# One block for a whole transformer layer: the output projection joined to attention, feed-forward weights into freed buffers

## The chip, the core and the metric

The kernel runs on one core of a Trainium2 chip. The core has five engines that work through their own instruction lists: TensorE (PE in the profile) multiplies matrices, VectorE (DVE), ScalarE (ACT) and GpSimd (POOL) work element by element, SyncE (SP) issues transfers here. They wait for each other through semaphores. The metric is device time in microseconds (us) of one execution.

## The reference, cut to what matters

```python
# x: 2 x 1024 x 512, 32 heads of 16, feed-forward width 1376, all float32
x = x + _layernorm(attention(_layernorm(x)))
x = x + _layernorm(feed_forward(_layernorm(x)))
# attention: q, k, v from w_attn, rope, causal softmax, y = probs @ v,
#            y += gating * softmax(q @ ak) @ av  (10 adapter tokens), then y @ w_proj.T
# feed_forward: (silu(x @ W_gate.T) * (x @ W_up.T)) @ W_down.T
```

## The kernel before, in words

Every matrix product that needs float32 precision is made of three: both operands are split into a high part and a low part, and high times high, high times low and low times high are added (lines 72 to 74, `split_matmuls`). ACT mostly makes the high part with a copy, DVE the low part with a subtraction.

The kernel has four stages. `stage_inputs` normalizes x and makes q, k, v and the adapter's part (`ya`) in four blocks of 512 rows. `stage_attention` goes through 16 groups of four heads; PE makes row maxima ahead of time, scores (L917) and products with v (L931), ACT takes the exponentials (L800), POOL masks the diagonal (L773). The two stages share one block of code. Each group ends with a copy of the unnormalized sums to DRAM (`y_heads`), whose last row of each head is the softmax's denominator. In the attention stage the four operand buffers `q_op`, `k_op`, `vg` are used in turn by the groups.

`stage_project` has a block of its own, so all engines meet at a barrier ahead of it. It works on 8 pieces of 256 rows. For piece m the steps are, in order:

- **load**: SP loads `y` (four transfers), two slices of the feed-forward weights (`raw`, 520 KB each), the adapter's part `ya_sb`, and x (`xr`).
- **spread** (PE, L1161): the inverse denominators `inv`, times a matrix of ones (`heads`), give a full tile `ps_r`; **divide** (DVE, L1124) multiplies y by it.
- **add** (POOL, L1079) adds the adapter's part; **high** (ACT, L1099) and **low** (DVE, L1136) split y into `y_h` and `y_l`.
- **project** (PE, L72 to L74): 24 matmuls into `ps_o`.
- **statistics** (DVE, L1143 to L1151), **power** (POOL, L1083 and L1085) for one over the deviation, **normalize** (ACT, L1113) into `z`, **residual** (POOL, L1090, z plus x), **store** (SP) to `x1` in DRAM.

Beside that ACT (L1105) and DVE (L1128) split two weight slices with every piece, so that after 8 pieces all 33 column blocks of the feed-forward weights are in `w_ffn_high` and `w_ffn_low`. `ps_r`, `ps_o`, `y`, `y_h`, `y_l` and `z` have two buffers each. The steps are written as a software pipeline, and DVE does for each turn: statistics of the piece before, divide of the next, two weight slices, low of the next.

`stage_feed_forward` is another block behind another barrier. It takes four blocks of 512 rows, the first of them straight from `z`. DVE and POOL normalize it, PE transposes it into `ps_f` (L1388), ACT and DVE split it (L1278, L1326), and then for each of 11 slices f PE makes `ps_g`, `ps_u` and the part of `ps_d` from the slice before. The next block's front is made beside that.

## Time and profile before

| | us |
|---|---|
| median of 3 runs (lowest, highest) | 1250.85 (1249.85, 1255.54) |
| the profiled execution | 1256.06 |
| its span, first to last instruction | 1254.4 |
| PE busy in the span | 1134.4 |
| DVE busy | 713.2 |
| ACT busy | 515.3 |
| POOL busy | 266.7 |

All durations in this document's prediction come from the profiled execution. A busy PE isn't a PE at its best: matmul ends are modelled, and the granted clock (1.00 is 2.4 GHz, 0.50 is 1.2 GHz) is shown apart. Times of an instruction are counted from the span's start. Behind a row of the timeline stands in brackets how long the engine had been idle before it, and what released it.

### The profile page before, as it was taken

What the parts mean: (1) busy time and instruction counts of PE and PEld (TensorE: products, weight loads), DVE (VectorE), ACT (ScalarE), POOL (GpSimd) and SP (SyncE); (2) the same over time, 40 slices, a digit from 0 to 9 for tenths busy, and PEclk for the clock granted to TensorE, in tenths of its full rate; (3) what the DMA queues carried; (4) which work ended last, traced back from release to release, by engine and by line L of the source; (5) the groups of instructions that cost most, each with busy time, mean ns of one, the idle gap of its engine ahead of it and who ended that gap; (6) DMA issues with size and microseconds to landing.
All of it is one profiled execution on the core that took longest, in us unless ns stands there. A gap on an engine that the chain in (4) does not pass through costs nothing. (4 is left out here: it accounts for less than half of the span.)

```text
span 1254.4 us, 18586 instructions
## 1 busy us (share of the span) xinstructions
PE 1134.4 (90%) x7036; PEld 770.0 (61%) x7036; DVE 713.2 (57%) x955; ACT 515.3 (41%) x1058; POOL 266.7 (21%) x260
## 2 busy tenths in 40 slices
PE   3999999898999999999999976775999999999996
PEld 1878778544545455545554335654887887887884
DVE  4756747767888788777876107972324324324324
ACT  3233233246777777777776533432111112111111
POOL 3525538101311112111111103651001001001001
PEclk9999999668999999999998677886999999999998
DMA  6356786544434445544400037962001101101100
GB/s 237 91 148 178 162 179 168 104 103 77 79 78 78 79 88 96 95 82 83 92 27 19 18 101 210 291 200 100 1 1 35 66 1 38 65 1 36 66 1 34
DMA packets 82522, 113.10 MB, mean 90 GB/s; under 512 B 24964, under 2 KB 42500, under 8 KB 82436
## 3 DMA queue, kind: packets, MB, share of 16 engines
q1 hardware_dynamic: 80580, 108.21, 33.6%
q10 hardware_dynamic: 1856, 3.71, 1.7%
q8 instruction: 58, 0.95, 0.3%
q14 instruction: 28, 0.23, 0.1%
HBM read 68.83 MB, written 42.21 MB: 89 GB/s over the span
## 5 line engine op out<-in xcount | busy, mean ns | idle before, releaser
L800 ACT ACTIVATE prob<-ps_s 128x512 f32<-128x512 f32 (+3 forms) x768 | 323.2, 497 | 167.6 <-PE ps_s L917 160.6
L820 DVE TENSOR_REDUCE neg<-ps_m 128x2 f32<-128x1024 f32 (+2 forms) x224 | 248.2, 1145 | 62.0 <-PE ps_m L882 40.0
L917 PE MATMUL ps_s<-q_op,k_op 50*128 50x512 f32 (+2 forms) x768 | 249.8, 459 | 18.0 <-ACT prob L800 13.2
L917 PEld LDWEIGHTS ps_s<-q_op,k_op 50*128 50x128 f32 x768 | 122.2, 196 | 125.3 <-ACT prob L800 60.9
L882 PE MATMUL ps_m<-k_op,q_op 48*128 48x512 f32 (+2 forms) x768 | 185.6, 420 | 9.8 <-DVE neg L820 6.8
L773 POOL TENSOR_SCALAR_AFFINE_SELECT prob<-prob 128x512 f32<-128x512 f32 x128 | 81.2, 634 | 429.3 <-ACT prob L800 429.3
L931 PE MATMUL ps_y<-prob,vg 128*17 128x512 f32 (+3 forms) x1536 | 160.9, 542 | 0.0
L1342 DVE TENSOR_TENSOR hf<-sl,ps_u 128x512 f32<-128x512 f32 (+1 forms) x44 | 30.2, 686 | 190.7 <-PE ps_u L74 190.7
L820 DVE TENSOR_REDUCE neg_far<-ps_m 128x4 f32<-128x512 f32 (+2 forms) x96 | 100.2, 1048 | 29.4 <-PE ps_m L887 27.9
L1411 PE MATMUL ps_d<-w_ffn_high,wp_high 128*128 128x512 f32 (+1 forms) x352 | 115.5, 391 | 0.0
L882 PEld LDWEIGHTS ps_m<-k_op,q_op 48*128 48x128 f32 x768 | 97.0, 198 | 28.9 <-DVE neg L820 20.1
L887 PE MATMUL ps_m<-causal_h,ident_h 64*128 64x128 bf16 x1024 | 99.6, 232 | 0.0
L931 PEld LDWEIGHTS ps_y<-prob,vg 128*17 128x17 f32 x1536 | 37.2, 102 | 81.8 <-issue 39.6
L1293 ACT ACTIVATE wp_high<-hf 128x512 fp32r<-128x512 f32 (+1 forms) x44 | 27.8, 632 | 131.5 <-DVE hf L1342 131.5
L1290 ACT ACTIVATE sl<-ps_g 128x512 f32<-128x512 f32 (+1 forms) x44 | 26.2, 596 | 133.7 <-PE ps_g L74 133.6
L1411 PEld LDWEIGHTS ps_d<-w_ffn_high,wp_high 128*128 128x128 f32 (+1 forms) x352 | 66.1, 188 | 15.0
L72 PE MATMUL ps_g<-x2T_h,w_ffn_high 128*128 128x512 f32 (+1 forms) x176 | 71.9, 408 | 2.2 <-DVE wp_low L1326 1.5
L72 PE MATMUL ps_u<-x2T_h,w_ffn_high 128*128 128x512 f32 (+1 forms) x176 | 70.0, 398 | 0.9 <-DVE hf L1342 0.9
L74 PE MATMUL ps_g<-x2T_h,w_ffn_low 128*128 128x512 f32 (+1 forms) x176 | 70.3, 399 | 0.0
L74 PE MATMUL ps_u<-x2T_h,w_ffn_low 128*128 128x512 f32 (+1 forms) x176 | 69.3, 394 | 0.0
L1411 PE MATMUL ps_d<-w_ffn_low,wp_high 128*128 128x512 f32 (+1 forms) x176 | 68.9, 392 | 0.0
L1266 POOL TENSOR_TENSOR d_rs<-d_ve,minus_half 128x4 f32<-128x4 f32 x4 | 4.0, 1006 | 275.8 <-DVE d_ve L1365 275.8
(161 smaller groups left out, 1757.5 us busy)
## 6 DMA issues: line engine op xcount, KB each, us to landing
raw<-in_w_ffn SPq DMA_DIRECT2D x16, 520.0 KB, 6.3
y_heads<-y_sb SPq DMA_DIRECT2D x32, 256.0 KB, 2.1
k_op<-k_parts SPq DMA_DIRECT2D x28, 256.0 KB, 4.3
q_op<-q_parts SPq DMA_DIRECT2D x56, 128.0 KB, 5.0
v_groups<-v_out SPq DMA_DIRECT2D x16, 272.0 KB, 4.1
x<-in_x SPq DMA_DIRECT2D x4, 1024.0 KB, 7.9
q_parts<-part_h SPq DMA_DIRECT2D x16, 256.0 KB, 2.9
q_parts<-part_l SPq DMA_DIRECT2D x16, 256.0 KB, 2.9
```

Source lines behind the costliest of these rows:

```text
L72: nc.tensor.matmul(out, lh, rh, start=k == 0, stop=False)
L74: last = nc.tensor.matmul(out, ll, rh, start=False, stop=k == len(pairs) - 1)
L773: pool.affine_select(out=diag, in_=diag, compare_op=ALU.is_ge, fill=0.0, base=0, pattern=[[0, HG], [1, P]], channel_multiplier=-1).then_in ...
L800: act.activation(prob[:, v % NPROB, h, unit_cols(u)], ps_s[:, y % NS, unit_cols(u)], ACT.Exp, scale=D ** -0.5).then_inc(s_exp, 1)
L820: nc.vector.tensor_reduce(to[:, :, pairs[0]:pairs[-1] + 1, i - TT * c], scores, axis=AX.X, op=ALU.max, negate=True).then_inc(a_read, 1)
L882: last = nc.tensor.matmul(ps_m[:, g % 2, s, base:base + wide], q_op[buf][r, c, pair, (i - TT * c) * P:(i - TT * c + 1) * P], k_op[buf][r, ...
L887: last = nc.tensor.matmul(ps_m[:, g % 2, s, diag:diag + P], ident_h[r, half], causal_h[r, half], start=False, stop=half == 1)
L917: nc.tensor.matmul(ps_s[:, y % NS, lo:BLK], k_op[buf][r, pair, j * P:(j + 1) * P], q_op[buf][r, c, pair, lo:BLK], start=True, stop=True)\
L931: last = nc.tensor.matmul(ps_y[32 * h:32 * h + VW, unit_cols(u)], vg[n % NBUF][:, j, h * VW:(h + 1) * VW], prob[:, v % NPROB, h, unit_cols ...
L1293: act.activation(hT_h[0:w, s], hf[0:w, s], ACT.Copy).then_inc(h_high[s], 1)
L1342: nc.vector.tensor_tensor(hf[0:w, s], sl[0:w, s], ps_u[0:w], op=ALU.mult).then_inc(h_mul[s], 1)
L1411: last = nc.tensor.matmul(ps_d[:, tt], a[0:w, s, q], b[0:w, cols], start=f == j == 0, stop=f == NF - 1 and j == 2)
```

## The change

The whole kernel becomes one block without barriers, and the loops of the last two stages are written out. `stage_project` is cut up: its steps become methods of a class `Tail`. Pieces 0 to 3 (the first batch) are written at the end of the attention stage's lists, pieces 4 to 7 in a new `stage_project`.

- Weights are loaded in 33 pieces of 128 columns (256 KB). 0 to 11 are loaded on SP in the last three groups, and split on DVE alone (a copy and a subtraction), each set of four in the operand buffer that a group has freed. 12 to 19 go beside pieces 4 to 7, two for each, 20 to 32 beside the first feed-forward block, on ACT and DVE.
- The first batch's `y`, `ya`, x and denominators are loaded on SP in group 13; its inverses are taken and placed in group 14.
- Normalize moves from ACT to DVE; the residual is shared by POOL and DVE, half each.
- Pieces 0 to 3 all use one `ps_r` and one `ps_o`; pieces 4 to 7 use two in turn.
- DVE finishes pieces 0 and 1 two turns late (`finish(m - 2)`). From piece 3 on the statistics of a piece come in the same turn as its project.
- The second batch's inverses are loaded, taken and placed between pieces 2 and 4.
- The first feed-forward block is now rows 0 to 511, read back from DRAM into `x1_first`, and its normalization is done beside piece 6.

```diff
 # stage_attention, SP, in the loop over the groups n
+            if n == NG - 3:
+                sp.wait_ge(wp_low, 1)
+                for i in range(4):
+                    tail.load_weights(sp, i)
...
+                tail.load_sums(sp, 0)
+                tail.load_y(sp, 0)
+                tail.load_y(sp, 1)
+                tail.load_ya(sp, 0)
+                tail.load_x(sp, 0)
+            if n == NG - 1:
+                for i in range(8, 12):
+                    tail.load_weights(sp, i)
...
+            if n == NG - 2:
+                tail.place_inverses(sp, 0)
+                for i in range(4, 8):
+                    tail.load_weights(sp, i)
 # stage_attention, POOL, behind the last group
+        for m in range(NP // B):
+            tail.add_adapter(pool, m)
+            if m:
+                tail.inverse_deviation(pool, m - 1)
+                tail.residual_pool(pool, m - 1)
 # stage_attention, DVE, behind the last maximum
+        tail.invert(dve, 0)
+        def weights(group, pieces):
+            dve.wait_ge(pv, NU * (group + 1))
+            for i in pieces:
+                tail.weights_high(dve, i)
+                tail.weights_low(dve, i)
+        def finish(m):
+            tail.statistics(dve, m)
+            tail.normalize(dve, m)
+            tail.residual_dve(dve, m)
+        weights(NG - 4, range(4))
+        weights(NG - 3, range(4, 8))
+        weights(NG - 2, range(8, 12))
+        for m in range(NP // B):
+            tail.divide(dve, m)
+            if m > 1:
+                finish(m - 2)
+            tail.low(dve, m)
+        finish(2)
 # stage_attention, PE, behind the last product
+        for m in range(NP // B):
+            for half in range(2):
+                tail.spread(pe, m, half)
+            if m:
+                for part in range(4):
+                    tail.project(pe, m - 1, part)
 # class Tail
+    def load_x(self, sp, m):
+        if m:
+            sp.wait_ge(self.x1_pool, m)
+            sp.wait_ge(self.x1_dve, m)
...
+    def store_x1(self, sp, m):
+        sp.wait_ge(self.x1_pool, m + 1)
+        sp.wait_ge(self.x1_dve, m + 1)
...
+    def spread(self, pe, m, half):
+        if half == 0:
+            pe.wait_ge(self.inv_in, 16 * HB * (m // (NP // B) + 1))
+            back = 1 if m <= NP // B else 2
+            if m > NP // B or 0 < m < NP // B:
+                pe.wait_ge(self.y_div, m - back + 1)
...
+    def project(self, pe, m, part):
+        k, half = divmod(part, 2)
+        if part == 0:
+            pe.wait_ge(self.y_low, m + 1)
+            back = 1 if m <= NP // B else 2
+            if m > NP // B or 0 < m < NP // B:
+                pe.wait_ge(self.z_norm, m - back + 1)
...
 # the new stage_project, SP
+        tail.load_x(sp, 3)
+        tail.load_y(sp, 5)
+        tail.load_ya(sp, 4)
+        tail.place_inverses(sp, 1)
+        tail.store_x1(sp, 3)
+        tail.load_x(sp, 4)
+        tail.load_weights(sp, 12)
+        tail.load_weights(sp, 13)
...
 # POOL
+        tail.inverse_deviation(pool, 3)
+        tail.add_adapter(pool, 4)
+        tail.residual_pool(pool, 3)
...
 # ACT
+        for m in last_m:
+            for i in range(2 * (m - 4) + 12, min(2 * (m - 4) + 14, LATE_WEIGHTS)):
...
+                tail.weights_high_act(act, i)
+            tail.high(act, m)
...
 # DVE
+        tail.invert(dve, 1)
+        tail.statistics(dve, 3)
+        tail.normalize(dve, 3)
+        tail.residual_dve(dve, 3)
+        tail.divide(dve, 4)
+        for m in last_m:
+            for i in range(2 * (m - 4) + 12, min(2 * (m - 4) + 14, LATE_WEIGHTS)):
+                tail.weights_low(dve, i)
+            tail.low(dve, m)
+            if m + 1 < NP:
+                tail.divide(dve, m + 1)
+            if m == NP - 2:
+                tail.f_stats(dve, 0)
+            tail.statistics(dve, m)
+            if m == NP - 2:
+                tail.f_normalize(dve, 0)
+            tail.normalize(dve, m)
+            tail.residual_dve(dve, m)
+            if m == NP - 1:
+                for c in range(CC):
+                    tail.f_low_of(dve, 0, c)
```

How instructions stand in a row is shown at three places. The first is DVE in the middle of the projection. Before (one turn of the written loop; `w_ffn_low` are the weights, `y_l` is low, `p_st` to `p_ve` the statistics, `y<-y,ps_r` divide; register work left out by starting behind it):

```order
456 L1143 BN_STATS p_st<-ps_o 128x6 [waits o_step,o_ps1]
457 L1143 BN_STATS p_st<-ps_o 128x6
458 L63 REGISTER_ALU [waits z_ready1]
459 L1148 BN_AGGR p_mv<-p_st 128x2 [waits o_step]
460 L1148 BN_AGGR p_mv<-p_st 128x2
461 L1149 REGISTER_ALU
462 L1150 TENSOR_SCALAR p_mm<-p_mv 128x2 [waits o_step]
463 L1151 TENSOR_SCALAR p_ve<-p_mv 128x2
464 L1123 REGISTER_ALU [waits y_in1]
465 L1124 TENSOR_TENSOR y<-y,ps_r 128x1024 [waits over_ps]
466 L1126 ISA
467 L1128 ISA [waits f_high]
```

The changed kernel's DVE in piece 5 (`z<-ps_o` is normalize, `z<-z,xr` DVE's half of the residual):

```order
504 L1181 TENSOR_TENSOR w_low_2192<-raw,w_high_2191 128x512 [waits fw_high_act]
505 L1181 TENSOR_TENSOR w_low_2194<-raw,w_high_2193 128x512 [waits fw_high_act]
506 L1137 TENSOR_TENSOR y_l<-y,y_h 128x1024 [waits y_high]
507 L1133 TENSOR_TENSOR y<-y,ps_r 128x1024 [waits over_ps,y_in0]
508 L1145 BN_STATS p_st<-ps_o 128x6 [waits o_step,o_ps]
509 L1145 BN_STATS p_st<-ps_o 128x6
510 L1150 BN_AGGR p_mv<-p_st 128x2 [waits o_step]
511 L1150 BN_AGGR p_mv<-p_st 128x2
512 L1152 TENSOR_SCALAR p_ve<-p_mv 128x2 [waits o_step]
513 L1160 TENSOR_SCALAR z<-ps_o,p_mv,p_rs 128x512 [waits x1_out1,o_rstd]
514 L1160 TENSOR_SCALAR z<-ps_o,p_mv,p_rs 128x512
515 L1168 TENSOR_TENSOR z<-z,xr 128x512 [waits xr_in,z_norm]
```

Normalize and half of the residual now stand between the statistics of a piece and the low part of the next, and the statistics wait for the project of the same turn. The second place is SP between the batches, in the changed kernel:

```order
422 L1089 DMA ya_sb<-ya 128x4x256 [waits y_sum]
423 L1123 DMA inv<-sums 32x512 [waits inverse]
424 L1123 DMA inv<-sums 32x512
425 L1100 DMA x_dram<-z 128x2x512 [waits x1_dve,x1_pool]
426 L1095 DMA xr<-in_x 128x2x512 [waits x1_dve,x1_pool]
427 L1108 DMA raw<-in_w_ffn 128x4x128 [waits fw_low] x2
428 L1265 DMA x_first<-x_dram 128x4x512 [waits x1_out1,x1_out0]
```

Weight pieces 12 and 13 (row 427) stand behind the store of piece 3, which waits for POOL's and DVE's residual. The third is POOL there:

```order
103 L1194 TENSOR_TENSOR p_rs<-p_ve,minus_half 128x2 [waits z_norm,o_var]
104 L1188 TENSOR_TENSOR y<-y,ya_sb 128x1024 [waits yad_in,y_div]
105 L1201 TENSOR_TENSOR z<-z,xr 128x512 [waits xr_in,z_norm]
106 L1188 TENSOR_TENSOR y<-y,ya_sb 128x1024 [waits yad_in,y_div]
107 L1194 TENSOR_TENSOR p_rs<-p_ve,minus_half 128x2 [waits z_norm,o_var]
108 L1201 TENSOR_TENSOR z<-z,xr 128x512 [waits xr_in,z_norm]
```

Piece 3's half residual (row 105) stands behind piece 4's add, which waits for divide.

## Rows read from the trace of the kernel before

**Rows 1.** Stages: stretch, length, busy us (count) by engine, clock, DMA share, GB/s
```profile
690.00:738.00 48.00, 45.09 (x222) 16.05 (x221) 3.35 (x1) 26.63 (x66) 7.61 (x12) 0.68 0.05 17
738.00:865.00 127.00, 79.35 (x277) 61.15 (x274) 87.67 (x98) 40.08 (x45) 55.65 (x33) 0.77 0.66 204
```

**Rows 2.** Timeline of PE, attention's end to first project: start, us, instruction, idle
```profile
735.68 2.35 PE L931 MATMUL ps_y<-prob,vg 128*17 128x512 f32 x32
741.29 6.88 PE L1161 MATMUL ps_r<-inv,heads 96*128 96x256 f32 x16 [3.27 <-PEq L1485]
759.60 0.80 PE L72 MATMUL ps_o<-wp_high,y_h 128*128 128x512 f32 x1 [11.43 <-DVE y_l L1136]
```

**Rows 3.** Timeline of PE, last project to first feed-forward matmul
```profile
843.64 0.40 PE L74 MATMUL ps_o<-wp_high,y_l 128*128 128x512 f32 x1
...
861.18 1.97 PE L1388 MATMUL ps_f<-ident,z 128*128 128x128 f32 x8 [0.56 <-DVE wp_low L1326]
864.64 0.79 PE L72 MATMUL ps_g<-x2T_h,w_ffn_high 128*128 128x512 f32 x1 [1.49 <-DVE wp_low L1326]
```

**Rows 4.** Timeline of DVE across attention's end, and SP's first projection load
```profile
714.22 3.35 DVE L860 RECIPROCAL sums<-sums 64x512 f32<-64x512 f32 x1 [31.19 <-DMA sums<-y_heads]
...
741.26 2.68 SPq L1036 DMA_DIRECT2D y<-y_heads  x4
```

**Rows 5.** Groups by shape, 738 to 865: busy, mean ns, idle before, releaser
```profile
L1128 DVE TENSOR_TENSOR w_ffn_low<-raw,w_ffn_high 128x1040 f32 x12 | 27.5, 2334 | 0.0
...
L1143 DVE BATCH_NORM_STATS2 p_st<-ps_o 128x6 f32<-128x512 f32 x16 | 10.3, 681 | 5.5 <-PE ps_o L74 5.5
L1124 DVE TENSOR_TENSOR y<-y,ps_r 128x1024 f32<-128x1024 f32 x8 | 9.8, 1219 | 31.8 <-DMA y<-y_heads 31.8
L1099 ACT ACTIVATE y_h<-y 128x1024 fp32r<-128x1024 f32 x8 | 8.5, 1059 | 19.4 <-POOL y L1079 19.4
...
L1083 POOL TENSOR_TENSOR p_rs<-p_ve,minus_half 128x2 f32<-128x2 f32 x8 | 5.7, 708 | 25.1 <-DVE p_ve L1151 25.1
L1128 DVE TENSOR_TENSOR w_ffn_low<-raw,w_ffn_high 128x1040 fp32r<-128x1040 f32 x4 | 5.0, 1242 | 4.9 <-ACT w_ffn_high L1105 4.8
```

**Rows 6.** Single lines: duration min/median/max in ns, first and last start, form
```profile
L1136 DVE TENSOR_TENSOR y_l<-y,y_h x8: 1152/3200/3259, 758.4 to 833.4; 128x1024 fp32r<-128x1024 f32 x8
...
L1079 POOL TENSOR_TENSOR y<-y,ya_sb x8: 2361/2979/3229, 753.9 to 829.3; 128x1024 f32<-128x1024 f32 x8
...
L1270 POOL TENSOR_TENSOR inv<-inv x4: 1260/1288/1297, 964.5 to 1246.5; 128x512 f32<-128x512 f32 x4
```

**Rows 7.** Timeline of DVE: normalizing in the feed-forward stage, and the residual
```profile
856.62 1.92 DVE L1320 TENSOR_SCALAR z<-z,f_mv,f_rs 128x512 f32<-128x512 f32 x4 [1.23 <-POOL f_rs L1261]
...
963.54 1.53 DVE L1370 TENSOR_SCALAR inv<-ps_d,d_mv,d_rs 128x512 f32<-128x512 f32 x2 [1.22 <-POOL d_rs L1266]
965.20 1.16 DVE L1375 TENSOR_TENSOR inv<-inv 128x512 f32<-128x512 f32 x1
```

**Rows 8.** Timeline of PE: project behind a wait, and behind hardly any
```profile
793.46 0.80 PE L72 MATMUL ps_o<-wp_high,y_h 128*128 128x512 f32 x1 [3.19 <-DVE y_l L1136]
...
801.64 1.89 PE L1161 MATMUL ps_r<-inv,heads 96*128 x8
804.32 0.50 PE L72 MATMUL ps_o<-wp_high,y_h 128*128 128x512 f32 x1 [0.79 <-DVE y_l L1136]
...
810.00 1.24 PE L1161 MATMUL ps_r<-inv,heads 96*128 x5
...
815.09 0.50 PE L72 MATMUL ps_o<-wp_high,y_h 128*128 128x512 f32 x1 [3.20 <-DVE y_l L1136]
...
822.31 1.89 PE L1161 MATMUL ps_r<-inv,heads 96*128 x8
```

**Rows 9.** DMA issues: how often, KB each, median us from issue to landing
```profile
raw<-in_w_ffn SPq DMA_DIRECT2D x16, 520.0 KB, 6.3
...
k_op<-k_parts SPq DMA_DIRECT2D x28, 256.0 KB, 4.3
```

863 lines of the change are left out of this document (462 added, 401 removed).

## The prediction

> **What bounds the kernel now.** I read the stages first [rows 1], then the timeline at the stages' ends [rows 2, 3], then the groups and single lines inside the projection [rows 5, 6], because the change leaves the instructions of the stages ahead of and behind it as they are, and PE is the bound there. Between the last attention product's end (735.7 + 2.35 = 738.0) [rows 2] and the first feed-forward matmul (864.6) [rows 3] lie 126.6 us, in which PE is busy for 79 at a mean clock of 0.77 and DVE for 88 [rows 1]. This is what can change. It has three parts: 21.6 us until the first project starts (759.6) [rows 2], 84.4 us for eight projects (the last ends at 844.0), so about 10.8 for each piece, and 20.6 us until feed-forward [rows 3]. In the first part the reader sees a barrier of 3.3 us and y's transfers issued only behind it [rows 2, 4]. In the second DVE has 87.7 of 127 busy, much of it prolonged: a weight subtraction takes 1.24 us alone and 2.33 in the loop, the low part 1.15 alone and 3.20 mostly, while POOL works beside it [rows 5, 6]. The third is a chain over normalize, residual, a barrier, statistics and transposes.
>
> **Part 1, attention's end to the first project.** The inverses, y, adapter part and x of piece 0 are there before 738, and no barrier stands ahead. DVE's split of weight pieces 0 to 11 comes in before: it is idle for 31.2 us ahead of the reciprocal at 714.2, and again until 747.7 [rows 4]. A piece is a copy and a subtraction of 512 columns, each about half of 1.24 us, so 12 x 1.25 = 15 us go into more than 50 idle ones: no cost; if that cover were gone, at most these 15. SP issues some 16 more transfers in group 13 at 0.67 us for each of y's (four in 2.68 [rows 4]), about 10 us, ahead of a store and the maxima's placing. Those are not needed for another half group: no cost taken, 3 us at most. Then the chain is spread 1.9 [rows 8], divide 1.2 [rows 5], add 2.5 (least 2.36, median 2.98 [rows 6]; nothing competes, so near the least), high 1.1 [rows 5], low 1.15 [rows 6], and 0.1 for each of five handovers: 8.4. Project 0 starts at 746.4, 13.2 us earlier than before.
>
> **Part 2, pieces 0 to 3.** Project's length depends on the clock. Behind an idle PE of 3.2 us it took 8.2 and 7.2 (793.46 to 801.64, 815.09 to 822.31); behind 0.8 us it took 5.7 (804.32 to 810.00) [rows 8]. There is no weight work on DVE here, but one `ps_r` and one `ps_o` tie the steps into a ring: project m+1 waits for normalize m, spread m+3 stands on PE behind project m+1, divide m+3 waits for it, and the statistics of m+1 stand on DVE behind that divide. So from one project's start to the next: project 7.7 (the mean of the two, as PE idles some 5 us in each turn), spread 1.9, divide 1.2, statistics 1.85 (two of 0.68 and three short ones; 0.17 taken for each), power 0.7, two normalizations 1.55 [rows 5, 7], handovers 0.4: 15.3 us, against 10.8 before. Two such turns bring project 2 to 777.0. The next has no spread and divide in it: 12.2, project 3 at 789.2.
>
> **Part 3, from the first batch to the second.** Project 3 is followed by statistics, power, normalize and DVE's half residual (1.15 [rows 7]): 13.4, so 802.6. Only then DVE divides piece 4 (1.2), POOL adds (2.5) and only behind that does its half of piece 3's residual (1.3 [rows 6]); with handovers 807.9. SP waits for that before it stores piece 3, loads x, and issues weight pieces 12 and 13: 1.9 us of issuing, then 4.3 until a load of 256 KB lands (6.3 for the 520 KB of before [rows 9]): 814.1. ACT copies weights (0.55) and makes the high part (1.06), DVE the low (1.15), handovers 0.3: project 4 starts at 817.2, 28.0 after project 3. SP's invert chain (reciprocal 3.35 [rows 4]) runs beside project 3.
>
> **Part 4, pieces 4 to 7.** PSUM is double here, but on DVE the statistics of piece m stand ahead of the low part of m+1, and wait for project m. The turn is project 7.7, statistics 1.85, power 0.7, normalize 1.55, residual 1.15, two weight subtractions 1.3, low 1.15, handovers 0.5: 15.9. All of it is one chain, PE and DVE never working at the same time except for a divide. Projects 5 and 6 start at 833.1 and 849.0. In the next turn the first feed-forward block's four normalizations (1.92 [rows 7]) take the place of the wait for power: 16.9, project 7 at 865.9.
>
> **Part 5, to feed-forward.** The first block's normalization is over, so its transposes follow project 7, the first two at once. The third waits for a low part that DVE does behind piece 7's statistics, normalize and residual: 7.7 + 5.7 = 13.4, then 0.7, then 3.5 as from the third transpose to the first matmul before (861.2 to 864.6) [rows 3]: 883.5. From the last project's end that is 9.9 us, where it was 20.6.
>
> **Sum.** Until the first project 13.2 us are gained and behind the last 10.7. From the first project's start to the last one's end it takes 873.6 - 746.4 = 127.2 in place of 84.4, which loses 42.8. Together +18.9 (883.5 - 864.6), taken as +19. Feed-forward is the same list on PE. Its 13 late weight pieces are at most 13 x 1.2 = 16 us of copies and subtractions, two engines together, beside the first block's PE work, a quarter of 1254.4 - 864.6, so 97 us: no cost taken, and 16 if nothing hid them. The profiled execution of 1256.06 would become 1275; it lies 5.2 above the median of 1250.85, so the median becomes 1270.
>
> **A rule beside it.** The Trainium skill, page "TensorE: Matmul & The Clock Gate", section "HAM oscillation — how this bites in real kernels", describes a loop whose every burst of matmuls starts at half clock because of the wait ahead of it; rows 8 agree for projects behind 3.2 us. Against that, the section "What's actually happening" of the same page puts the clock's ramp at under 1% of a typical kernel's span. As an estimate that would be at most 12.5 us here, where eight projects at 7.7 in place of 5.6 cost 16.8; by that rule the sum would be at least 4 us smaller.
>
> **Rivals.** *B, full clock.* If PE's waits of some 5 us don't lower the clock, each project takes 5.6 and all eight lie on the path: 16.8 less, +2.2, so 1253. For it: the project at 804.3 ran at 5.7 [rows 8]. Against it: 3.2 us were enough twice, and all waits get longer. *C, DVE and POOL in each other's way.* The gains on DVE rest on subtractions at their short length. If in pieces 4 to 7 POOL's work falls beside low and weights, low takes 3.2 (+2.05 x 4), each weight 1.16 instead of 0.65 (+0.5 x 8) and adds 3.0 (+2): +14, so 1284. Against it: by the rings POOL is done by then. The Trainium skill, "SBUF — State Buffer", section "Who interferes with whom", makes this a lock between GpSimd reads and a DVE instruction with two SBUF inputs, which fits 1152 against 3200 ns [rows 6]. *D, faster.* The clock is the one mechanism that could do it, from the last attention group on: from 690 to 738 PE was busy for 45.1 us at 0.68 [rows 1]. At full clock this is 30.7, and ACT's 26.6 would fit. If the regrouped program kept the clock up from there through the projection, attention would end 14 us earlier and B's +2 would follow: -12, so 1239. It decides, with projects at 5.6, as soon as attention ends before 729.5 (2.2 + 6.3 earlier). Against it: PE's list in the last group is unchanged. *E, the change doesn't do what it says:* the early weights aren't ready by 738, because SP or the subtractions are late, and DVE does up to 15 us of them ahead of divide 0: up to +34, 1285.
>
> **How the numbers follow.** Forecast 0.64, B 0.10, C 0.14, D 0.08, E 0.04. The forecast's own terms reach from 1262 (projects at 7.2, landings of 3 us) to 1278 (8.2, landings of 6.3). The range from 1253 to 1288 takes in B, C and E's bound and leaves out D. A measurement of this kernel tells about 0.5%, 6 us, from no change. Faster by more: D and the lower end of B, 0.10. Within: most of B and the forecast's lowest end, 0.12. Slower: 0.78.
>
> **What the profile after would show.** Right: project 0 at about 746, projects 15 apart in the first batch, 28 from project 3 to 4, then 16 apart; DVE waits for PE's `ps_o` ahead of each statistics and PE for `y_l`; clock near 0.7 from 738 to 880; weight pieces 0 to 11 subtracted before 738; first feed-forward matmul at about 884. Wrong: if PE waits for a transfer of y or ya in each turn, if projects run at 5.7, or if attention's end moves by more than 3 us, a term above is mis-sized.

## Result: 1269.5 us, 1.4% slower, and the profile after

The changed kernel takes 1269.5 us (median of 4 runs, 1269.0 to 1271.7), the kernel before 1251.6 (1249.9 to 1255.5 in the same comparison). The ratio is 1.0142, 95% interval 1.0119 to 1.0165, so 17.9 us slower. The profiled execution took 1269.63 us, its span 1267.9. The stages by time in the profile after, as [rows 1] of before (columns: stretch, its length, then busy time and count of PE, PE's weight loads, DVE, ACT and POOL, then PE's granted clock, DMA share and GB/s):

```profile
690.00:738.00 48.00, 45.08 (x223) 16.19 (x222) 10.08 (x18) 26.88 (x66) 7.87 (x12) 0.68 0.20 58
738.00:880.00 142.00, 81.45 (x276) 62.67 (x264) 64.12 (x99) 14.86 (x19) 37.20 (x24) 0.75 0.42 130
880.00:1268.00 388.00, 370.63 (x1640) 302.43 (x1640) 129.68 (x219) 69.97 (x116) 19.51 (x17) 0.98 0.12 39
```

Attention is as before: 10 us of DVE's weight work have come into the last 48, and PE's row is the same. In the 142 us behind it PE has 81 busy and DVE 64, which is 57% and 45% of the stretch, where [rows 1] have 62% and 69%: both stand more. PE's timeline of the changed kernel shows the start of the eight projects (`ps_o`), the first spread of each batch (`ps_r`; x16 are two spreads in a row), and the start of feed-forward, as [rows 2, 3] do for before (columns: start, us, engine, line, operation, tile<-operands, count, idle before and who ended it):

```profile
738.20 1.99 PE L1223 MATMUL ps_r<-inv,heads 96*128 96x256 f32 x8
...
746.35 0.50 PE L1238 MATMUL ps_o<-wp_high,y_h 128*128 128x512 f32 x1 [2.72 <-DVE y_l L1137]
...
759.45 0.77 PE L1238 MATMUL ps_o<-wp_high,y_h 128*128 128x512 f32 x1 [5.63 <-DVE z L1160]
...
775.16 0.77 PE L1238 MATMUL ps_o<-wp_high,y_h 128*128 128x512 f32 x1 [5.64 <-DVE z L1160]
...
786.95 0.76 PE L1238 MATMUL ps_o<-wp_high,y_h 128*128 128x512 f32 x1 [4.41 <-DVE z L1160]
...
799.57 6.87 PE L1223 MATMUL ps_r<-inv,heads 96*128 96x256 f32 x16 [4.35 <-DMA inv<-sums]
...
818.17 0.79 PE L1238 MATMUL ps_o<-wp_high,y_h 128*128 128x512 f32 x1 [11.73 <-DVE y_l L1137]
...
834.65 0.80 PE L1238 MATMUL ps_o<-wp_high,y_h 128*128 128x512 f32 x1 [6.72 <-DVE y_l L1137]
...
851.43 0.79 PE L1238 MATMUL ps_o<-wp_high,y_h 128*128 128x512 f32 x1 [6.72 <-DVE y_l L1137]
...
869.26 0.80 PE L1238 MATMUL ps_o<-wp_high,y_h 128*128 128x512 f32 x1 [9.36 <-DVE y_l L1137]
...
886.73 0.79 PE L76 MATMUL ps_g<-x2T_h,w_high 128*128 128x512 f32 x1 [1.41 <-DVE x2T_l L1410]
```

Ahead of each of projects 1 to 7 PE idles 4.4 to 11.7 us, and it is always DVE that ends this wait: `z` (normalize, the ring) in the first batch, `y_l` (the low part) in the second. Only the wait ahead of the second batch's first spread (799.57) is ended by a DMA. Against the forecast:

| | predicted | measured |
|---|---|---|
| project 0 | 746.4 | 746.35 |
| steps 0-1, 1-2, 2-3 | 15.3, 15.3, 12.2 | 13.1, 15.7, 11.8 |
| step 3-4 | 28.0 | 31.2 |
| steps 4-5, 5-6, 6-7 | 15.9, 15.9, 16.9 | 16.5, 16.8, 17.8 |
| project 7 to feed-forward | 17.6 | 17.5 |
| first feed-forward matmul | 883.5 | 886.73 |
| feed-forward to the end of the span | 389.8 (as before) | 381.2 |

So the stretch up to feed-forward is 22.1 us longer than before, 3.2 more than forecast, and feed-forward is 8.6 us shorter, of which the prediction has nothing.

### The profile page after: what moved, and what is told of

The parts are those of the page before. It is cut to its first block and busy times, and to the rows that moved or that the text cites. A ratio compares the mean times of both kernels' runs of the same rounds, so it can differ in the third digit from the quotient of the medians.

```text
span 1267.9 us, 18066 instructions
## 1 busy us (share of the span) xinstructions
PE 1131.8 (89%) x7020; PEld 771.7 (61%) x7020; DVE 707.8 (56%) x983; ACT 494.1 (39%) x1042; POOL 249.7 (20%) x251
## 5 line engine op out<-in xcount | busy, mean ns | idle before, releaser
L1550 PE MATMUL ps_d<-w_high,wp_high 128*128 128x512 f32 (+1 forms) x352 | 115.0, 390 | 0.0
L1238 PE MATMUL ps_o<-wp_high,y_h 128*128 128x512 f32 x64 | 33.2, 519 | 52.9 <-DVE y_l L1137 37.3
L1550 PEld LDWEIGHTS ps_d<-w_high,wp_high 128*128 128x128 f32 (+1 forms) x352 | 66.1, 188 | 14.0
L76 PE MATMUL ps_g<-x2T_h,w_high 128*128 128x512 f32 (+1 forms) x176 | 70.8, 402 | 1.4 <-DVE x2T_l L1410 1.4
L76 PE MATMUL ps_u<-x2T_h,w_high 128*128 128x512 f32 (+1 forms) x176 | 68.9, 391 | 1.2 <-DVE hf L1485 1.2
L78 PE MATMUL ps_g<-x2T_h,w_low 128*128 128x512 f32 (+1 forms) x176 | 69.3, 394 | 0.0
L78 PE MATMUL ps_u<-x2T_h,w_low 128*128 128x512 f32 (+1 forms) x176 | 68.6, 390 | 0.0
L1550 PE MATMUL ps_d<-w_low,wp_high 128*128 128x512 f32 (+1 forms) x176 | 68.5, 389 | 0.0
```

Source lines behind the costliest of these rows:

```text
L76: nc.tensor.matmul(out, lh, rh, start=k == 0, stop=False)
L78: last = nc.tensor.matmul(out, ll, rh, start=False, stop=k == len(pairs) - 1)
L1238: last = self.nc.tensor.matmul(self.ps_o(m)[:, k], a[:, s, c, q], b[:, c], start=c == x == 0, stop=c == CC - 1 and x == 2)
L1550: last = nc.tensor.matmul(ps_d[:, tt], a[0:w, i % 2, q], b[0:w], start=f == j == 0, stop=f == NF - 1 and j == 2)
```

## Experiments on the clock and on the waits of the projection

Each kernel was timed against the kernel before on its own chip. A change against the changed kernel is worked out from the quotient of the two ratios, times 1269.5; from the two 95% intervals such a difference is uncertain by some 4 to 5 us either way. Edits are to the changed kernel unless it is said otherwise.

**PE kept busy in its waits.** Ahead of projects 1 to 7 stand 6 to 20 matmuls of no use.

```diff
+    def keep_busy(self, pe, m, times):
+        ...                                    # behind low m-1 (and normalize m-1)
+        for _ in range(times):
+            self.nc.tensor.matmul(out, self.heads[:, 0:P], self.inv[0:KR, 0:W], start=True, stop=True)
...
+                tail.keep_busy(pe, m - 1, 20 if m == 5 else 11)
                 for part in range(4):
                     tail.project(pe, m - 1, part)
```

> The changed kernel with 6 to 20 idle matmuls (heads by the inverses, 256 columns, results overwritten) ahead of projects 1 to 7, in the time in which PE waited: nothing else is moved. Theory K (the length of a project is the clock's, and the clock falls in the waits of some 5 us): projects 1 to 7 take 5.6 to 5.7 us in place of 7.4 to 8.3, the clock between 738 and 880 is above 0.9 in place of 0.75, and as each project lies on the chain the kernel is 7 x 2.4 = 17 us faster than the changed one, about 1253. Rival D (PE's length doesn't matter, DVE's and POOL's work bound the turns, so only the waits get longer): under 4 us faster. Rival F (idle matmuls delay the projects as much as they speed them up): within 5 us of the changed kernel, with projects at 5.7 that start later in their turns.

Measured: 1259.6 us, ratio 1.0056 [1.0039, 1.0072]: 10.8 us faster than the changed kernel. Its window behind attention, and PE at the start of projects 1 and 2 and at the spread of the second batch:

```profile
738.00:880.00 142.00, 109.87 (x437) 89.34 (x438) 67.79 (x105) 16.50 (x22) 37.11 (x24) 0.88 0.46 143
...
752.85 0.47 PE L1249 MATMUL ps_o<-wp_high,y_h 128*128 128x512 f32 x1 [2.17 <-DVE z L1162]
...
765.91 0.76 PE L1249 MATMUL ps_o<-wp_high,y_h 128*128 128x512 f32 x1 [2.18 <-DVE z L1162]
...
790.43 1.19 PE L1225 MATMUL ps_r<-inv,heads 96*128 96x256 f32 x2 [7.38 <-DMA inv<-sums]
```

The clock rose from 0.75 to 0.88; from the first project's start to feed-forward it is 0.89 against 0.72. Projects 1, 3 and 5 ran at full clock throughout (5.7 us), while 2, 4, 6 and 7 took 7.0 to 7.4. Project 2 started at half clock behind the same wait of 2.2 us as project 1: the 752.85 matmul takes 0.47 us, that at 765.91 takes 0.76. Projects 6 and 7, behind 1.98 and 2.45 us, started at full clock and fell to half of it within their first 1.6 us: in project 6 a matmul of 0.41 us is followed by one of 0.60, and those behind take 0.63.

```profile
840.17 0.41 PE L1249 MATMUL ps_o<-wp_high,y_h 128*128 128x512 f32 x1
840.40 0.60 PE L1249 MATMUL ps_o<-wp_low,y_h 128*128 128x512 f32 x1
```

The lengths let the theory be tested piece by piece. Against the changed kernel, projects 1, 2 and 4 to 7 were shorter by 2.66, 0.36, 0.69, 2.59, 1.09 and 0.71 us, and the steps that begin with them (project 7's up to feed-forward) by 2.65, 0.36, 0.68, 2.59, 1.09 and 0.71: one for one. Project 3 was shorter by 2.56 and its step longer by 0.8: there PE waits for the second batch's inverses. So K holds as to the mechanism, and D and F fall by these steps. Its size of 17 did not come: the extra matmuls don't hold the clock up each time, and one project of seven isn't on the chain. In the profile the steps add up to 7.3 us; its attention also ended 6.6 us earlier than in the changed kernel's profile, with the same instructions on PE, so what the 10.8 us hold beyond 7.3 isn't shown to come from the projects.

**Weights 12 and 13 first.**

```diff
     def _(sp):
+        tail.load_weights(sp, 12)
+        tail.load_weights(sp, 13)
         tail.load_x(sp, 3)
         ...
         tail.load_x(sp, 4)
-        tail.load_weights(sp, 12)
-        tail.load_weights(sp, 13)
```

> The changed kernel, with the loads of weight pieces 12 and 13 issued at the head of the second batch, ahead of piece 3's x, in place of behind piece 3's store. In the changed kernel it took 31.2 us from project 3 to project 4, against 12 to 16 for the others. Theory T (the chain through POOL's residual, the store and the weights' landing sets project 4): the high part and the subtractions no longer wait for a landing; add 4 and then the low part set it. Project 4 starts 8 us earlier, at about 810, and the whole is 8 us faster, about 1261. Rival V (divide, add 4 and the low part behind it end last anyway): project 4 moves by less than 2 us, and the time stays at 1268 to 1270.

Measured: 1266.6 us, 1.0106 [1.0088, 1.0124]: 4.5 us faster, between the two. PE in the second batch's first spread and in project 4:

```profile
803.66 5.78 PE L1223 MATMUL ps_r<-inv,heads 96*128 96x256 f32 x16 [8.84 <-DMA inv<-sums]
...
814.35 0.80 PE L1238 MATMUL ps_o<-wp_high,y_h 128*128 128x512 f32 x1 [4.91 <-DVE y_l L1137]
```

Step 3-4 fell from 31.2 to 26.7 only, less than the 8 us of theory T and more than V's 2, and step 4-5 grew from 16.5 to 18.6. The two loads stand on SP ahead of the placing of the inverses, which is issued 2.1 us later (795.08 against 792.95): the spread waits 8.84 us for them where it waited 4.35. A transfer moved forward on a queue pushed back the one that was nearly as late.

**Weights and inverses both early.** Weights 12 and 13 are loaded first, as in the last run, and the second batch's sums are loaded, inverted and placed beside pieces 0 and 1, and no longer beside piece 3.

```diff
         store_y(NG - 1, 1)
+        for c in range(HB):
+            sp.wait_ge(y_out[c], 16 * NG)
+        tail.load_sums(sp, 1)
         tail.load_ya(sp, 1)
         tail.load_y(sp, 2)
+        tail.place_inverses(sp, 1)
...
             tail.low(dve, m)
+            if m == 1:
+                tail.invert(dve, 1)
```

> The changed kernel with two things moved ahead: weight pieces 12 and 13 are loaded ahead of x of piece 3, and the sums of the second batch are loaded, inverted and placed beside pieces 0 and 1 in place of beside piece 3. With the weights alone project 4 came 26.7 us behind project 3 (31.2 in the changed kernel), and spread 4 waited 8.8 us for the inverses, which landed 4 us later than before. Theory I (the inverses' landing was the second wait, right behind the weights'): spread 4 stands ready behind project 3, DVE's divide 4 follows residual 3 at once, and project 4 comes 19 to 20 us behind project 3: 11 to 12 us off the changed kernel, about 1258. Rival V (POOL's residual and add, or landings of x and y, end last anyway): the step stays above 24.

Measured: 1260.4 us, 1.0057 [1.0028, 1.0085]: 10.6 us faster. PE, then DVE and POOL of this kernel:

```profile
794.50 3.62 PE L1226 MATMUL ps_r<-inv,heads 96*128 96x256 f32 x16
806.40 0.79 PE L1241 MATMUL ps_o<-wp_high,y_h 128*128 128x512 f32 x1 [8.28 <-DVE y_l L1140]
...
800.71 3.43 DVE L1184 TENSOR_TENSOR w_low<-raw,w_high 128x512 fp32r<-128x512 f32 x2
...
801.31 2.83 DVE L1184 TENSOR_TENSOR w_low<-raw,w_high 128x512 fp32r<-128x512 f32 x1
...
800.90 2.69 POOL L1191 TENSOR_TENSOR y<-y,ya_sb 128x1024 f32<-128x1024 f32 x1 [3.53 <-DVE y L1136]
```

The spreads follow project 3 with no wait and at full clock (3.62 us for both in place of 6.87), and project 4 comes 20.0 us behind project 3. Theory I holds to the microsecond, and rival V falls. Some of it is given back by a longer step 4-5 (18.9 in place of 16.5): POOL's add of piece 5 waits for the adapter part until 816.35, and ACT for the weights until 819.47. The last three rows show a collision: of two weight subtractions the first takes 0.69 us, and the second, begun when POOL's add was running (row 801.31), takes 2.83. It isn't what sets project 4, since DVE then still waits 0.57 us for ACT's high part.

**Two banks from the start.**

```diff
-        self.ps_r = lambda m: ps_r[m >= NP // B and m % 2 == 0][:]
-        self.ps_o = lambda m: ps_o[m >= NP // B and m % 2 == 0][:]
+        self.ps_r = lambda m: ps_r[m % 2][:]
+        self.ps_o = lambda m: ps_o[m % 2][:]
```

The waits of spread m and project m follow (divide and normalize m-2), and PE waits once more ahead of spread 1, for the copies of the last attention sums out of PSUM (`y_ready`).

> The changed kernel, with the second ps_r and ps_o used by pieces 0 to 3 too: project m+1 no longer waits for normalize m, nor spread m+1 for divide m. Theory R (in the first batch the one ps_o ties project, statistics, power, normalize into a ring): steps from project to project in pieces 0 to 3 fall from 13.1, 15.7, 11.8 to about 10 to 12, project 3 starts 9 us earlier, at about 780 where it was 787; as the inverses of the second batch then land earlier only by the half of it, 5 us of it reach feed-forward: about 1264.5. Rival Q (DVE's list, in which statistics m-2 stand between divide m and low m, sets the pace with any number of banks): the steps stay above 13 and the time within 2 us of the changed kernel.

Measured: 1263.6 us, 1.0087 [1.0059, 1.0115]: 6.9 us faster. Steps 9.0, 12.4, 11.8, then 35.5: project 3 starts at 778.3, 8.6 us earlier than in the changed kernel (7.4 of it by the steps, the rest by attention's end), and 4.3 of it are given back in the step behind it, where the spreads stand waiting for the inverses. Theory R holds, and Q falls: of Q's steps above 13 none is left.

**Statistics one turn later, in pieces 4 to 7.**

```diff
             if m + 1 < NP:
                 tail.divide(dve, m + 1)
+            if m > 4:
+                tail.statistics(dve, m - 1)
+            if m + 1 < NP:
+                weights_and_low(m + 1)
-            tail.statistics(dve, m)
-            tail.normalize(dve, m)
-            tail.residual_dve(dve, m)
+            if m > 4:
+                tail.normalize(dve, m - 1)
+                tail.residual_dve(dve, m - 1)
```

> The changed kernel, with statistics, power, normalize and residual of pieces 4 to 7 one turn later on DVE (POOL and SP follow), so that the two subtractions and the low part of the next piece stand ahead of them. Theory O (DVE's order makes a turn the sum of project, statistics, normalize, subtractions and low): the steps 16.5, 16.8, 17.8 of pieces 4 to 7 fall to 11, 12.5 and 15.6, less where weights land late; the last piece's finish comes in full behind project 7, which gives back some; together 5 us off: 1264.5. Rival W (the weights' landings bound the turn, as SP issues two of them behind each piece's y): steps stay above 15, the gain is under 2 us or a loss.

Measured: 1258.8 us, 1.0056 [1.0036, 1.0076]: 10.8 us faster. Steps 11.1, 12.5 and 16.5, where it was 16.5, 16.8, 17.8: theory O to within 1 us for each, and W falls. From project 7 to feed-forward it takes 18.9 in place of 17.5, as piece 7's finish stands in full behind it. The gain is larger than the 5 expected, since that end gives back 1.4 us only, where the expectation (12 us off the steps, 5 in all) had counted some 7.

**The three together**, the edits of the last three at once.

> The changed kernel with the edits of the double banks, of the late statistics and of the two things moved early, all at once, but still in two batches with SP's, POOL's and DVE's lists as they were. Apart they took 6, 11 and 11 us off. Theory S (they undo three different waits in three stretches, so they add up, and somewhat more, as the inverses no longer cap what the double banks gain): the steps are about 10, 12, 12 | 20 | 11, 12.5, 16 and the first feed-forward matmul comes at about 860, the whole at 1240: the remaining 37 us down to the kernel with one pattern of turns come from the turn itself (one weight piece a turn, statistics behind the next low part in all eight, no step between batches, finish behind the transposes). Rival T (the waits hide each other, what one frees the other takes): no more than 15 us off the changed kernel, about 1254.

Measured: 1245.8 us, 0.9959 [0.9924, 0.9993]: 22.9 us faster than the changed kernel, where the three apart make 28.3; with some 5 us of uncertainty the times don't tell these two apart. It is more than T's 15 and short of S's 1240. The steps are 9.0, 12.5, 11.8 | 23.7 | 16.4, 12.6, 16.7. The first batch's steps are those of the double banks alone. The step between the batches and the next one fell short of the 20 and 11 expected, and POOL and ACT show what they wait for:

```profile
796.64 2.34 POOL L1193 TENSOR_TENSOR y<-y,ya_sb 128x1024 f32<-128x1024 f32 x1 [8.19 <-DMA ya_sb<-ya]
...
814.14 1.38 ACT L1218 ACTIVATE w_high<-raw 128x512 fp32r<-128x512 f32 x2 [14.08 <-DMA raw<-in_w_ffn]
```

Now the adapter part of piece 4 is late (SP issues it behind weights, x and four loads of y), and then weights 14 and 15. SP's list was made for the old pace.

**One pattern of turns for all eight pieces.**

```diff
+        for t in range(NP):                        # DVE
+            if t + 1 < NP:
+                tail.divide(dve, t + 1)
+            ...
+            if t:
+                tail.statistics(dve, t - 1)
+            ...
+            tail.weights_low(dve, EARLY_WEIGHTS + t)
+            if t + 1 < NP:
+                tail.low(dve, t + 1)
+            ...
+            if t:
+                finish(t - 1)                      # normalize, residual
...
+        for m in range(NP):                        # PE
+            if m == NP - 1:
+                for c in range(2):
+                    tail.f_transposes(pe, 0, c)
+            for part in range(4):
+                tail.project(pe, m, part)
+            if m + 2 < NP:
+                spread(m + 2)
```

> All that the runs before showed to hold up the chain, undone at once in the changed kernel: two ps_r and ps_o from piece 0 on, one pattern of turns for all eight pieces (no second batch), spread m+2 right behind project m, statistics, normalize and residual of piece m-1 behind the divide and the low part of piece m+1, one weight piece a turn in place of two, the second batch's inverses and weights 12 to 15 loaded right behind attention, the first feed-forward block's first two transposes ahead of project 7 and piece 7's finish behind its low parts. Theory (the turn is then the longer of project with spread, 7.7 + 1.9 = 9.6 cold and 7.6 warm, and of DVE's list, 1.2 + 1.85 + 0.65 + 1.2 + 1.55 + 0.7 = 7.2, with POOL's 2.4 + 0.7 + 1.8 beside it): steps of 8 to 10 us, project 7 at 808 to 815, the first feed-forward matmul at about 822, where the kernel before has 864.6, and feed-forward 381 as in the changed kernel: 1200 to 1210. Rival C (DVE and POOL, now at work side by side in every turn, stretch each other: low 2.1 to 3.2 in place of 1.2, subtraction 1.2 in place of 0.65, add 3): turns of 11, feed-forward at 840, about 1222. Rival L (a landing of y, ya or x of 4 to 6 us behind a store becomes the ring: x of piece m is loaded only behind residual m-1 and its store): turns of 13 and 1235.

Measured: 1203.5 us (1201.3 to 1206.0), 0.9591 [0.9569, 0.9613]: 4.1% faster than the kernel before, 69 us faster than the changed one. The stretch from its first project to feed-forward (ahead of it the same stretch of the three edits together), and PE at projects 1, 2, 5 and 6 and at feed-forward:

```profile
744.40:865.80 121.40, 72.93 (x257) 57.51 (x257) 64.31 (x104) 14.50 (x19) 37.91 (x24) 0.75 0.49 151
```

```profile
743.90:819.30 75.40, 62.65 (x256) 49.85 (x256) 63.23 (x97) 13.85 (x19) 38.93 (x22) 0.93 0.68 215
...
755.24 0.50 PE L1212 MATMUL ps_o<-wp_high,y_h 128*128 128x512 f32 x1 [1.91 <-DVE y_l L1113]
...
763.22 0.47 PE L1212 MATMUL ps_o<-wp_high,y_h 128*128 128x512 f32 x1 [0.50 <-DVE z L1136]
...
787.87 0.47 PE L1212 MATMUL ps_o<-wp_high,y_h 128*128 128x512 f32 x1 [0.70 <-DVE z L1136]
...
799.91 0.76 PE L1212 MATMUL ps_o<-wp_high,y_h 128*128 128x512 f32 x1 [4.59 <-DVE z L1136]
...
819.31 0.50 PE L76 MATMUL ps_g<-x2T_h,w_high 128*128 128x512 f32 x1 [1.93 <-DVE x2T_l L1384]
```

Steps are 11.3, 8.0, 8.1, 8.4, 8.1, 12.0 and 10.9; PE waits 0.5 to 1.0 us in the middle ones, all projects from 1 to 5 run in 5.7 us, and the clock is 0.93. The theory holds in the middle turns and for feed-forward (8 to 10 and 822 expected), and rivals C (turns of 11) and L (13) fall; the first turn and the last two are longer than 10. Where DVE does the first block's statistics PE waits 4.6 us, and project 6 starts at half clock (0.76).

From the first project to feed-forward this kernel takes 75.4 us, the three edits together 121.4. The clock of the projects is the smaller part of these 46 us: the eight projects take 50.5 us here and 60.1 there, so 9.5 us. The step between the batches (23.7, now 8.4) makes 15.3, the stretch behind project 7's start (18.7, now 8.5) 10.2, and both hold some of the 9.5; the other 20.5 us lie in the other turns, in their projects and in their waits. Which of the regrouped lists gave how much wasn't measured apart.

## Experiments on feed-forward

These stand on the kernel before. First its loops written out:

```diff
-            with engine.Fori(0, NB // 2) as t:
+            for t in range(NB // 2):
```

> The kernel before, with the feed-forward's loop on each engine written out, every instruction kept. In the changed kernel feed-forward took 381.2 us from its first matmul to the end of the span, in the kernel before 389.8, which the prediction had not said. Theory L (the loops themselves, with the waits and addresses that come out of registers, cost it): feed-forward falls to about 382 to 384 us and the run is 6 to 8 us below the kernel before. Theory S (the kernel before normalizes and transposes a fifth block that nobody uses; the changed one doesn't): this run is within 2 us of the kernel before, and the gain is in the next one. Theory A (the share of the two is equal): 4 us below.

Measured: 1252.0 us, 0.9993 [0.9975, 1.0011]. Feed-forward 387.9 us in the profile, so 1.9 less, which the times can't tell from nothing. Theory L falls. Then without the fifth block:

```diff
-                front(n + 1, 1 - k)
+                if n + 1 < NB:
+                    front(n + 1, 1 - k)
```

> As the last, and without the loads, statistics, normalization and transposes for the fifth block that is never multiplied (they change no output). Theory L: no more than 1 us below the written-out loops alone. Theory S: 16 transposes and their waits go from the last block, whose length was 105.6 us from its first matmul to the end in the kernel before and 102.1 in the changed one: 3.5 us below the run before it. Both theories: feed-forward is then as long as in the changed kernel, 381 us; if it stays above 385, the gain has a third cause.

Measured: 1248.5 us, 0.9971 [0.9958, 0.9983]: 3.5 us below the last by the medians, 2.8 by the ratios, give or take 2.7. Feed-forward itself is 1.7 shorter (386.2), half of what theory S had. Above 385, so there is a third cause. PE's rate pointed to the operands' places: the gate and up weights packed piece by piece,

```diff
-                cols = [slice(base + c * F + f * P, base + c * F + f * P + FW[f]) for c in range(CC)]
+                cols = [slice(at, at + FW[f]) for at in (base + CC * f * P + c * FW[f] for c in range(CC))]
```

> The kernel before with the loops written out and the fifth block left out, as in the last of these, and one thing more: the gate and up weights lie in SBUF piece by piece (the four 128-column tiles of a piece next to each other, as in the changed kernel) in place of row by row (the tiles of a piece 5504 bytes apart). The written-out loops took 1.9 us off feed-forward (387.9) and the fifth block 1.7 (386.2); the changed kernel stands at 381.2, with 12 matmuls of ps_g or ps_u in 2.72 us against 2.79. Theory P (where the tiles lie sets the rate at which PE takes the matmuls): ps_g and ps_u fall to 2.72 per 12, feed-forward to 381 to 382, the whole to about 1244. Rival R (the rate comes from something else that regrouping moved, such as the place of x2T or of the weights as a whole): the 12 stay at 2.79 and the time within 1.5 us of 1248.5.

then x2T moved by 128 bytes,

```diff
+        sb("pad", [P, 32])
         xT_h = sb("x2T_h", [P, 2, CC, BLK], F32R)
```

> The kernel with the packed weights, and x2T_h and x2T_l moved up by 128 bytes a partition by an unused tensor ahead of them. With the packed weights 12 matmuls of ps_g or ps_u took 2.75 us in feed-forward blocks 0 and 2 (whose low part lies in wp_low, at byte 25248) and still 2.79 in blocks 1 and 3 (low part in x2T_l, at 203808); in the changed kernel it is 2.72 in all four. There all operands, weights and x2T alike, start at 160 past a multiple of 512 bytes; in the packed kernel the weights and wp_low do, and x2T_h and x2T_l stand at 32 past it. Theory A (weights and moving operand at the same place within 512 bytes go at the faster rate): 2.72 in all four blocks, feed-forward 381 to 382 us in place of 384.8, 3 us faster. Rival R (another property of the place): 2.75 and 2.79 stay, the time within 1.5 us.

and last, on top of both, the weights moved by 384 bytes; x2T behind them moves along, so that both stand at 32 past a multiple of 512:

```diff
+        ctx.enter_context(nc.sbuf_tensor("pad_w", [P, 96], F32))
         w_all = [ctx.enter_context(nc.sbuf_tensor(f"w_ffn_{part}", [P, W_ALL], F32R)) for part in ("high", "low")]
```

> The kernel with packed weights once more, with the weights moved by 384 bytes, so that weights and x2T all start at 32 past a multiple of 512 bytes, while wp_low (low part of blocks 0 and 2) and wp_high (the hidden part of ps_d) stay at 160 past it. Theory M (the fast rate needs weights and moving operand at the same place within 512 bytes, whichever it is): 2.72 us per 12 matmuls of ps_g and ps_u in blocks 1 and 3, about 2.75 in blocks 0 and 2, ps_d 2.74 to 2.76. Rival Q (160 past it is a good place, and 32 a bad one): 2.79 or more in blocks 1 and 3.

Measured (the times of 12 matmuls are medians within a block, from start to start in PE's timeline):

| kernel | us | ratio to before | feed-forward | 12 of `ps_u`, blocks 0 and 2 | blocks 1 and 3 | 12 of `ps_d` |
|---|---|---|---|---|---|---|
| before | 1251.6 | | 389.8 | 2.79 | 2.80 | 2.74, 2.75 |
| written out | 1252.0 | 0.9993 | 387.9 | 2.79 | 2.80 | 2.74, 2.75 |
| no fifth block | 1248.5 | 0.9971 | 386.2 | 2.78, 2.79 | 2.80 | 2.74, 2.75 |
| packed | 1248.0 | 0.9973 [0.9954, 0.9992] | 384.8 | 2.75 | 2.80 | 2.74, 2.76 |
| packed, x2T at 160 | 1242.8 | 0.9926 [0.9897, 0.9954] | 382.0 | 2.72 | 2.72 | 2.72 |
| packed, all but wp at 32 | 1246.6 | 0.9966 [0.9934, 0.9997] | 386.1 | 2.77, 2.81 | 2.72 | 2.78 to 2.80 |
| changed kernel | 1269.5 | 1.0142 | 381.2 | 2.72 | 2.72 | 2.72 |

PE's timeline in the last block, first of the packed kernel, then of the one with x2T at 160, shows the single matmuls come 0.23 to 0.24 us apart in the first, and 0.22 to 0.23 in the second:

```profile
1200.63 0.40 PE L72 MATMUL ps_g<-x2T_h,w_ffn_high 128*128 128x512 f32 x1
1200.86 0.39 PE L73 MATMUL ps_g<-x2T_l,w_ffn_high 128*128 128x512 f32 x1
...
1202.02 0.40 PE L72 MATMUL ps_g<-x2T_h,w_ffn_high 128*128 128x512 f32 x1
```

```profile
1200.28 0.39 PE L72 MATMUL ps_g<-x2T_h,w_ffn_high 128*128 128x512 f32 x1
1200.51 0.39 PE L73 MATMUL ps_g<-x2T_l,w_ffn_high 128*128 128x512 f32 x1
...
1201.64 0.39 PE L72 MATMUL ps_g<-x2T_h,w_ffn_high 128*128 128x512 f32 x1
```

Six matmuls take 1.39 us in the first and 1.36 in the second. Packing alone made blocks 0 and 2 faster by half and left 1 and 3 as they were, so it lies between P and R. The next two say more. With all operands at 160, `ps_u` and `ps_d` go at 2.72 in all blocks, as theory A has it. With weights and x2T at 32 and both wp tensors left at 160, `ps_u` goes at 2.72 in blocks 1 and 3 too, whose operands are now all at 32, and where one of the two operands lies in wp (the low part of blocks 0 and 2, all of `ps_d`) the group is slow, 2.77 to 2.81. So Q falls: 160 isn't the good place and 32 the bad one. M holds only in part, since `ps_g` of blocks 1 and 3, for which it had 2.72 as well, takes 2.75 and 2.76. What unequal places cost is not settled: in blocks 0 and 2 eight unequal pairs of twelve made 2.75 in the packed kernel and four made 2.77 to 2.81 in the last. Nor is it shown that a group's own operands are all that counts: `ps_d` takes 2.74 to 2.76 in the packed kernel and 2.72 in the next, though its own two operands are at 160 in both; the pad moved x2T and with it all that is laid out behind. Only 32 and 160 were compared in this way.

In the changed kernel all pieces and x2T lie at 160 because one function lays them out one behind the other in freed buffers. So the 8.6 us are: the fifth block's work 1.7 in the profile, the operands' places 4.2 (386.2 to 382.0), the loops up to 1.9, and 0.8 that stay open, each from single profiles.

## Why the prediction was right, and where only by balance

The sign, the size and the place were right: 1270.0 predicted, 1269.5 measured. Point by point:

- **Part 1 held.** Project 0 at 746.35. The early weights were free: the last subtraction of pieces 0 to 11, on DVE of the changed kernel, comes 21 us ahead of attention's end, and rival E falls.

```profile
716.28 0.69 DVE L1181 TENSOR_TENSOR w_low<-raw,w_high 128x512 fp32r<-128x512 f32 x1
```

- **Part 2 held as a ring**, and taking the ring away moved what it should. One term was off: project 0 ran in 5.7 us, so project 1 came 2.2 us early. This was luck. PE had idled 2.72 us ahead of it, and behind the same 2.71 or 2.72 us, and with PE's list up to there unchanged, project 0 took 7.4 us in the profiles of weights 12 and 13 first, of both early and of the late statistics.
- **Part 3 had one wrong step.** "SP's invert chain runs beside project 3" put a price of nothing on it. In the changed kernel:

```profile
787.45 3.34 DVE L1128 RECIPROCAL sums<-sums 64x512 f32<-64x512 f32 x1
792.95 1.25 SPq L1123 DMA_DIRECT2D inv<-sums  x2
...
803.43 1.22 DVE L1133 TENSOR_TENSOR y<-y,ps_r 128x1024 f32<-128x1024 f32 x1 [3.22 <-PE ps_r L1223]
804.73 2.34 POOL L1188 TENSOR_TENSOR y<-y,ya_sb 128x1024 f32<-128x1024 f32 x1 [6.81 <-DVE y L1133]
807.03 1.26 POOL L1201 TENSOR_TENSOR z<-z,xr 128x512 f32<-128x512 f32 x1
...
809.24 1.61 SPq L1108 DMA_DIRECT2D raw<-in_w_ffn  x2
...
814.57 1.34 ACT L1213 ACTIVATE w_high<-raw 128x512 fp32r<-128x512 f32 x2 [34.27 <-DMA raw<-in_w_ffn]
```

  The reciprocal ends at 790.8, SP issues the placing behind four loads of y and one of ya at 792.95, the spread starts 799.57 and is done, at half clock, for the divide at 803.43: 16.5 us behind project 3, where the prediction had 13.4. From the divide on it took 14.7 against 14.6. The 3.1 us up to the divide are this step, and nearly all of the 3.2 by which step 3-4 was too short. In the chain shown, ahead of that divide, DVE had been idle for 3.22 us.
- **Part 4 was 0.6 to 0.9 us short a turn.** The residual half takes 0.69, not 1.15, and the project 8.0 to 8.5, not 7.7; and the two subtractions took 2.35, not 1.3, because POOL's residual half stands beside them. DVE and POOL of the changed kernel, in the turn of piece 5:

```profile
847.27 0.69 DVE L1168 TENSOR_TENSOR z<-z,xr 128x512 f32<-128x512 f32 x1
847.88 2.35 DVE L1181 TENSOR_TENSOR w_low<-raw,w_high 128x512 fp32r<-128x512 f32 x2
850.16 1.21 DVE L1137 TENSOR_TENSOR y_l<-y,y_h 128x1024 fp32r<-128x1024 f32 x1
...
847.32 1.76 POOL L1201 TENSOR_TENSOR z<-z,xr 128x512 f32<-128x512 f32 x1 [1.64 <-DVE z L1160]
```

  Two subtractions take 1.40 us in the turn of piece 4, where POOL stands still, so some 1 us of the 2.35 is POOL's instruction, which had begun first and ends at 849.08. That is rival C at a fifth of its price: some 1 us in each of three turns, not 14, since low and add came through at 1.2 and 2.4. The rule of the Trainium skill, "SBUF — State Buffer", section "Who interferes with whom" (a DVE instruction with two SBUF inputs contends with a GpSimd instruction that reads SBUF), agrees with these rows.
- **Rival B fell.** The projects took 5.7, 8.4, 7.4, 8.3, 8.0, 8.3, 8.5 and 8.1 us, 62.6 in all, where full clock would be 45.6 (eight at 5.7): 17.0 us for the clock, as the sum had it (16.8), and the run with PE kept busy shows for six of seven projects that they count one for one. But the length of the wait doesn't settle a project's clock, as the prediction took it from the three projects of [rows 8]. Two others of the kernel before, from first start to last end 5.9 and 7.4 us long, show it:

```profile
782.68 0.51 PE L72 MATMUL ps_o<-wp_high,y_h 128*128 128x512 f32 x1 [1.82 <-DVE y_l L1136]
783.03 0.39 PE L73 MATMUL ps_o<-wp_low,y_h 128*128 128x512 f32 x1
...
825.95 0.55 PE L72 MATMUL ps_o<-wp_high,y_h 128*128 128x512 f32 x1 [1.75 <-DVE y_l L1136]
826.30 0.63 PE L73 MATMUL ps_o<-wp_low,y_h 128*128 128x512 f32 x1
```

  The shorter wait has the slower project. And of the two projects behind 3.2 us in [rows 8] only the first starts at half clock (0.80 for its first matmul); the second starts at full clock (0.50) and is slow all the same, so these rows agree with a start at half clock for one project, not for both as the prediction says. So 7.7 for each came true as a mean of 7.8, while the wait alone doesn't tell a single project's length. The Trainium skill's estimate of under 1% of a typical kernel's span ("TensorE: Matmul & The Clock Gate", section "What's actually happening"), as an estimate at most 12.5 us here, is too small for this kernel, where 17.0 of 1267.9 us are 1.3%. The same page's section "HAM oscillation — how this bites in real kernels" describes bursts that each start at half clock behind a wait, and projects 1 to 7 do so here (first matmul 0.76 to 0.80 us, against 0.50 in project 0).
- **Rival D fell**: the granted clock from 690 to 738 is 0.68 again.
- **The step that failed is "feed-forward is the same list on PE".** The order of the instructions was the same; the places of their operands, and 16 transposes that nobody used, were not. It made 8.6 us, of which the experiments place 1.7 (the transposes) and 4.2 (the places) by single profiles. In the profiled execution the sum had given 1275, and 1269.6 came: +3.2 on the chain, -8.6 in feed-forward. That the median was hit to 0.5 us comes from a second error on the other side: I took 5.2 us off as the distance of the profiled execution from the median, and in the changed kernel that distance is 0.1. Nothing here shows where those 5 us came from. One thing that moves from profile to profile is attention's end: with its PE instructions unchanged, the first spread behind it started between 731.6 and 738.2 in the profiles of the changed kernel and its variants. So the hit to within 0.5 us is luck; what was right is the sign, the place, and the chain up to feed-forward to within 3.2 us of 18.9.

## What to carry to other kernels

Two batches joined in one program are not one pipeline: as long as banks, DVE's order and the loads keep their old pattern, an engine's wait per turn grows, and on PE such waits can cost twice, as projects behind them ran at the lower clock (7.4 to 8.5 us in place of 5.7). When a transfer is made earlier on a queue, name the transfer behind it that was nearly as late. "The same list of instructions" is not the same time: compare a matmul's spacing before and after as well, and where the operands lie.

## What the runs showed of the hardware that I had not expected

- Matmuls of 128x512 at full clock came 0.227 us apart (2.72 for 12) where all weights and moving operands of feed-forward start 160 bytes past a multiple of 512, and 0.228 to 0.234 apart (2.74 to 2.81) in nearly all groups of the kernels where some start elsewhere. Over this feed-forward it makes some 4 us of 386. The rule behind it is open.
- Extra matmuls in PE's waits raised the clock only in part: with 1.8 to 2.5 us of wait left ahead of them, projects 1, 3 and 5 ran in 5.7 us and 2, 6 and 7 in 7.0 to 7.4. The fall can come inside a project: in project 6 at 840.4, 1 us behind its start, when PE was no longer waiting.
- A DVE subtraction with both inputs in SBUF, started while a POOL addition that reads SBUF was running, lasted until 0.55 us behind the end of that one: 0.69 us became 1.75 beside a residual half of 1.76 (ended 849.08), and 2.83 beside an add of 2.69 (ended 803.59).
